# Five of the next batch's gate products moved from the mixing block into the woven block, and semaphores cleared beside later work

## The reference, cut to what matters

```python
# first mixer of a batch: projection and gate of the input x
xz = in_proj_w @ x                     # (2*1024) x 512 tokens: x part and gate part
x_part, z = split(xz)                  # z is used as silu(z), last of all
# second layer's mixer, per head, 512 steps:
kv = kt[..., :, None] * vt[..., None, :]
ot = einsum('bhk,bhkv->bhv', rt, S + bonus * kv);  S = S * dt[..., :, None] + kv
on = (o - mean) * rsqrt(var + EPS) * gn_w + gn_b
o = on * (gh * sigmoid(gh));  return o.reshape(...) @ Wo
```

## Time and profile before

| | us |
|---|---|
| median of three runs | 3989.97 (3979.78 to 3990.33) |
| profiled execution, time | 3982.17 |
| profiled execution, first to last instruction | 3980.4 |
| PE busy | 3521.7 (88%) |
| DVE busy | 3172.7 (80%) |
| ACT busy | 1609.0 (40%) |
| POOL busy | 1378.0 (35%) |
| a load of a ring slot, issue to landing, median | 4.2 |

### The profile page before, as it was taken

The page is one execution under the profiler, slowest core; times in us unless marked ns, Lnnn a source line. Parts: engine busy times, 40 slices in busy tenths (PEclk is TensorE's granted clock), DMA queues, the critical chain, the costliest instruction groups (busy, mean ns, idle before and its releaser), DMA issues. The chain is left out here.

```text
span 3980.4 us, 41707 instructions
## 1 busy us (share of the span) xinstructions
PE 3521.7 (88%) x15442; PEld 1475.8 (37%) x15442; DVE 3172.7 (80%) x2733; ACT 1609.0 (40%) x2189; POOL 1378.0 (35%) x493
## 2 busy tenths in 40 slices
PE   5777779989999979989999979989999988967999
PEld 1222243334333443334333443334433443324444
DVE  5999469887999869887999869887999869895333
ACT  5666343214655353214655353214655343213001
POOL 3454304362344304372344304372344304361000
PEclk9788899999899999989899999989899999978999
DMA  6678402121233302122233302122233302110222
GB/s 228 241 286 302 159 12 72 60 78 65 88 105 97 131 27 72 59 72 72 85 102 102 130 27 72 57 74 72 79 104 105 131 27 72 57 40 16 103 96 72
DMA packets 105431, 382.95 MB, mean 96 GB/s; under 512 B 14224, under 2 KB 27920, under 8 KB 102800
## 3 DMA queue, kind: packets, MB, share of 16 engines
q1 hardware_dynamic: 83632, 342.57, 24.6%
q10 hardware_dynamic: 21600, 37.73, 3.4%
HBM read 290.80 MB, written 64.32 MB: 89 GB/s over the span
## 5 line engine op out<-in xcount | busy, mean ns | idle before, releaser
L300 PE MATMUL ps<-r,ring 128*128 128x512 bf16 (+1 forms) x2040 | 781.4, 384 | 0.0
L297 PE MATMUL ps<-xr,ring 128*128 128x512 bf16 x1568 | 613.8, 391 | 1.4 <-PEq L2278 1.4
L301 PE MATMUL ps<-xr,ring 128*128 128x512 bf16 x1568 | 611.1, 390 | 0.0
L297 PE MATMUL ps<-r,ring 128*128 128x512 bf16 (+3 forms) x1384 | 545.4, 395 | 49.4 <-DVE xc L1102 17.8
L301 PE MATMUL ps<-r,ring 128*128 128x512 bf16 (+3 forms) x1384 | 544.8, 395 | 0.0
L1154 POOL TENSOR_TENSOR hh<-hh,bc 128x2048 f32<-128x2048 f32 x72 | 334.7, 4649 | 518.3 <-DVE hh L1064 518.3
L1154 POOL TENSOR_TENSOR bc<-bc 128x2048 f32<-128x2048 f32 x64 | 304.3, 4754 | 344.6 <-DVE bc L1064 344.6
L1154 POOL TENSOR_TENSOR r<-r,bc 128x2048 f32<-128x2048 f32 x56 | 260.9, 4658 | 297.7 <-DVE r L1064 297.7
L1064 DVE TENSOR_TENSOR_SCAN hh<-da,hh 128x2048 f32<-128x2048 f32 x72 | 325.7, 4523 | 1.3
L1105 DVE TENSOR_TENSOR xc<-xc,ps 128x512 f32<-128x512 f32 x176 | 119.5, 679 | 226.1 <-PE ps L301 225.8
L1064 DVE TENSOR_TENSOR_SCAN bc<-da,bc 128x2048 f32<-128x2048 f32 x64 | 296.0, 4625 | 0.5
(11 more groups left out here) (267 smaller groups left out, 6559.4 us busy)
## 6 DMA issues: line engine op xcount, KB each, us to landing
ring<-wsplit SPq DMA_DIRECT2D x216, 768.0 KB, 4.2
r<-wstream SPq DMA_DIRECT2D x54, 768.0 KB, 7.0
ring<-wsplit SPq DMA_DIRECT2D x76, 512.0 KB, 3.9
wsplit<-ring SPq DMA_DIRECT2D x38, 768.0 KB, 4.3
da<-r ACTq DMA_DIRECT2D x360, 63.9 KB, 2.1
wsplit<-r SPq DMA_DIRECT2D x14, 768.0 KB, 5.5
r<-wstream SPq DMA_DIRECT2D x19, 512.0 KB, 6.4
r<-xT SPq DMA_DIRECT2D x7, 1024.0 KB, 6.4
```

Source lines behind the costliest of these rows:

```text
L297: mm = pe.matmul(out, w_hi, x_hi, start=start, stop=False)
L300: pe.matmul(out, w_hi, x_lo, start=False, stop=False)
L301: return pe.matmul(out, w_lo, x_hi, start=False, stop=stop)
```

## The change

1. **Products.** The mixing block keeps 11 of the next batch's 16 products (eight projections, gates 0 to 2); gates 3 to 7 go to the woven block. There gates 3 and 4 stand where the 18 idle products were, and gates 5 to 7 where the 26 were. Behind them TensorE waits until ScalarE has taken all five. ScalarE does their curves behind the factor and ahead of the preparation's curve 2. SyncE stores them, behind the load of the second preparation slot, and ScalarE waits for the stores before it overwrites the region.
2. **Order in the scan steps.** The list of products is dealt out 3, 2, 2, 2, 3, 2, 2, 1 in place of 3, 2, 3, 3, 2, 3, 3, 3, and in group 1 two of them go ahead of the first reduce.
3. **GpSimd.** The four low parts of the next input stand behind its multiplies of groups 0 and 1, two and two, not ahead of them.
4. **Clears.** No blocks for them. A group's semaphores are cleared by SyncE alone at the start of the next block in which it streams weights, ahead of its loads; one block at the end of the kernel clears the last 41. The names carry a number, so that two groups can be held at once.

```diff
 def stream_block(k, sp, slots_end, last=NSLOTS):
+    for group, _ in k.stale:
+        for s in group:
+            sp.sem_clear(s)
+    k.idle += k.stale
+    k.stale = []
     k.w.load_until(sp, slots_end, RING - 1, last)
...
-            stream_block(k, sp, W_WO, last)
+            stream_block(k, sp, W_PROJ + 4 if ahead else W_WO, last)
...
-            work = [(value, 2), (value, 3)] + [(gate, o) for o in range(4)] + ([(ahead_product, n) for n in range(2 * J0)] if ahead else [])
+            work = [(value, 2), (value, 3)] + [(gate, o) for o in range(4)] + ([(ahead_product, n) for n in range(J0 + 3)] if ahead else [])
...
-                if g >= 1:
+                if g >= 2:
                     reduce(g - 1)
-                until = max(len(work) * (g + 1) // G, min(3, len(work)))
+                until = min(3 + 2 * g + g // 4, len(work))
...
+                if g == 1:
+                    reduce(g - 1)
...
-                for c in range(KM):
-                    low(pool, k.xn_lo[:, c, :], k.xn[:, c, :]).then_inc(nsplit, 1)
...
                 read_states(pool, g, 0, share(g)).then_inc(prod, 1)
+                if ahead and g < 2:
+                    for c in range(2 * g, 2 * g + 2):
+                        low(pool, k.xn_lo[:, c, :], k.xn[:, c, :]).then_inc(nsplit, 1)
...
-            stream_block(k, sp, W_MOE, last)
+            stream_block(k, sp, W_WO, last)
+            if ahead:
+                k.w.load_until(sp, W_WO + 2, RING - 1, last)
+                for j in range(3, J0):
+                    sp.wait_ge(gate_in, j - 2)
+                    sp.dma_start(k.gates_dram[:, j, :], k.dt0[:, j, :]).then_inc(gate_stored, 16)
+            k.w.load_until(sp, W_MOE, RING - 1, last)
...
-            keep_busy(k, pe, 0, 18)
+            if ahead:
+                gate(3)
+                gate(4)
+            else:
+                keep_busy(k, pe, 0, 18)
...
-            keep_busy(k, pe, 0, 26)
+            if ahead:
+                pe.wait_ge(cent, KM)
+                for j in range(5, J0):
+                    gate(j)
+                pe.wait_ge(gate_in, 5)
+            else:
+                keep_busy(k, pe, 0, 26)
...
             if ahead:
+                for j in range(3, J0):
+                    act.wait_ge(gate_mm, j - 2)
+                    act.activation(k.dt0[:, j, :], gate_bank(j), ACT.Silu).then_inc(gate_in, 1)
                 s.silu(act, 2)
...
                 s.take_low(act)
+                act.wait_ge(gate_stored, 5 * 16)
...
-                with nc.Block() as blk:
-                    @blk.gpsimd
-                    def _(pool):
-                        for s in held[0::4]:
-                            pool.sem_clear(s)
...
+            for _, done in k.idle:
+                done.close()
+            k.idle = []
+            k.stale.append((held, own))
...
+        with nc.Block() as blk:
+            @blk.sync
+            def _(sp):
+                for group, _ in k.stale:
+                    for s in group:
+                        sp.sem_clear(s)
```

More of the change, by code:

```diff
@@ L1489, in mix_batch @@
         bon, bv, osum, own_prod, gsplit, nsplit = sems("bon", "bv", "osum", "own_prod", "gsplit", "nsplit")
-        stored = sems("stored0", "stored1", "stored2", "stored3")
+        stored, = sems("stored")
         blk = ctx.enter_context(nc.Block())
@@ L1689, in _ @@
                     act.activation(k.projected[:, n, :], bank(N0 + n), ACT.Copy).then_inc(taken, 1)
-                for j in range(J0):
+                for j in range(3):
                     n = N0 + J0 + j
                     act.wait_ge(outp, n + 1)
-                    if j >= 4:
-                        act.wait_ge(stored[j % 4], 16)
                     act.activation(staged(j), bank(n), ACT.Silu).then_inc(taken, 1)
                     act.wait_ge(taken, n + 1)
-                    act.dma_start(k.gates_dram[:, j, :], staged(j)).then_inc(stored[j % 4], 16)
-                for i in range(4):
-                    act.wait_ge(stored[i], 32)
+                    act.dma_start(k.gates_dram[:, j, :], staged(j)).then_inc(stored, 16)
+                act.wait_ge(stored, 3 * 16)
         @blk.gpsimd
@@ L1838, in close_batch, with gate_bank @@
         logit_bank = k.ps[:, 0, 0:64].rearrange("p (c e) -> p c e", c=4)
+        gate_mm, gate_in, gate_stored = [sem(n) for n in ("gate_mm", "gate_in", "gate_stored")]
+        def gate_bank(j):
+            return k.ps[:, {3: 6, 4: 7, 5: 4, 6: 3, 7: 2}[j], :]
         def first_rows(engine, step):
@@ L1865, in mix, with gate @@
                     mm.then_inc(mixed, 1)
+            def gate(j):
+                wt = k.w.wait(pe, W_PROJ + 3 + j // 3)
+                for c in range(KM):
+                    mm = product(k, pe, gate_bank(j), wt, (j % 3 * KM + c) * P, P, high(k.xn[:, c, :]), k.xn_lo[:, c, :],
+                                 c == 0, c == KM - 1, tell=(c == 0))
+                mm.then_inc(gate_mm, 1)
+                if j in (5, 7):
+                    k.w.done()
             for c in range(KM):
@@ L2265, in cleared, with sem @@
         def cleared(order=None):
[L2267 to L2277, removed]
-                with nc.Block() as blk:
-                    @blk.gpsimd
-                    def _(pool):
-                        for s in held[0::4]:
-                            pool.sem_clear(s)
[L2284 to L2299, removed]
+            own, held, outer = ExitStack(), [], k.sem
+            def sem(name):
+                held.append(own.enter_context(nc.semaphore(f"{name}_{turn}")))
+                return held[-1]
+            k.turn += 1
+            turn = k.turn
+            if order is not None:
+                k.w = WeightStream(wsplit, ring, [sem(f"w_landed{i}") for i in range(RING)], sem("w_used"), order)
+            k.sem = sem
+            yield
+            k.sem = outer
+            for _, done in k.idle:
+                done.close()
+            k.idle = []
+            k.stale.append((held, own))
+        k.sem, k.stale, k.idle, k.turn = None, [], [], 0
         first_slots = [*range(W_PROJ, W_PROJ + 3), W_PREP0, W_PREP0 + 1]
@@ L2349, in decoder @@
         sequence(B - 1, False)
+        with nc.Block() as blk:
[4 more added lines that the diff above has]
+                        sp.sem_clear(s)
+        for _, done in k.idle + k.stale:
+            done.close()
 def _cols(a, n):
```

## The result

The changed kernel takes 3955.85 us (median; 3953.2 to 3958.3), the kernel before 3989.49 (3979.78 to 3990.33), measured together: ratio 0.992, 95% interval 0.991 to 0.994. The profiled execution took 3953.2 us with a span of 3951.4, against 3982.2 and 3980.4. The forecast was 3949, its sum for the profiled execution 3946.4.

What follows compares the result with a forecast made beforehand. It took TensorE's late last reduction to bound the mixing block's tail, and a chain the woven block's start. 3982.2 - 29.8 - 23.4 + 17.4 = 3946.4 profiled, 3954 by median; forecast 3949, a third between; range 3929 to 3971.

Steps and rivals of the forecast that it cites:

- Part 1: Block boundaries: clears and their barriers leave the path, hidden in SyncE's queue; 29.8 us saved.
- the cover: Feed-forward scan block: 12.8 us of slack in the queued load hides 79 clears (4.4 us) on SyncE.
- Part 2: Mixing block's scan: TensorE relieved of five products, GpSimd's multiply earlier; 7.8 us gained in each of three batches, 23.4.
- a share of 5.97: Mixing block: TensorE's first reduction waited 5.97 us for GpSimd's first multiply, behind low parts that the change moves.
- Part 3: Woven block: moved gates and their curves delay the first mixer product by 5.8 us, 17.4 lost over three batches.
- All behind it is one chain: Woven block: everything behind the mixer is one chain, so the mixer's 5.8 us delay is lost in each batch.
- One sign of being wrong: Time between successive woven block starts: 897.6 us before, 888 expected; over 893 would show the forecast wrong.
- 1 (the detour is hidden): Rival in the woven block: it hides its detour, the 5.8 us fall away, 3929.0 us; chance 0.11.
- 2: Rival in the mixing block: TensorE, or its clock, stays last and nothing is gained there; 3969.8 us, chance 0.14.
- 3: Rival on the clears: SyncE's serial run of clears makes loads late in most blocks; 3976.2 us, chance 0.07.
- 4: Rival in the scan steps: TensorE's clock falls to 0.5 throughout, making the kernel slower; 4030 us, chance 0.05.

Runs made afterwards that it cites:

- staggered: The changed kernel plus a block ahead of batches 0 to 2 in which SyncE clears an unused semaphore 20, 40 and 60 times; 3977.2 us, ratio 0.997.
- clears_only: The kernel before with only the clears moved as in the change; 3952.4 us, ratio 0.990.
- moves_only: The changed kernel with the clears as in the kernel before; 3988.5 us, ratio 1.001.
- after: The changed kernel itself, measured beside the kernel before; 3955.9 us, ratio 0.992.
- curve_first: The changed kernel with the preparation's curve 2 on ScalarE ahead of the five gate curves; 3928.8 us, ratio 0.985.
- thick_mixes: The changed kernel with one idle product after each of the twelve products of the mixing block's first three mixes; 3989.7 us, ratio 1.001.

## Why the forecast was 7 us low

The sum for the profiled execution was 3946.4, it took 3953.2. That the two are so near is in part luck: terms that were off by +16.5 and by -9.7 us stand against each other. Term by term:

**Part 1, the clears: right, with a gain beside it that no term had.** -29.8 forecast, -30.1 measured, and the cover held: 79 clears ahead of a load cost the feed-forward block nothing. The layer norm at the start of each batch was another 1.7 us shorter, 6.8 in all, at a clock of 1.00 for 0.89. It is 13.2 us in all four batches of every kernel without the clearing blocks except staggered, whose pauses of 2.95 and 3.66 us bring it back to 14.9 and 15.6; so it hangs on TensorE's idle time ahead of it, though its pause of 1.39 us (2.43 us idle) does nothing. clears_only gave 34.6 of median; it too has clock effects in both directions.

**Part 2, the scan: right in mechanism, small by 2.3 us a batch.** -7.8 forecast, -10.1 measured (83.3 to 73.2). moves_only, where the first half is as before, had 8.6 to 8.8. The other 1.4 are in the first step: in moves_only GpSimd's low parts of the gate's input still run beside the first scan (5.26 us), in after they were over by then and it took 4.42. The low parts of the next input, for which I took 0.8 us, cost nothing that shows. The Trainium skill, "SBUF — State Buffer", section "Who interferes with whom", has the later of the two engines wait for the whole instruction; the trace agrees: VectorE's read, begun at 1736.21 beside the multiply that ends at 1737.68, takes 2.54 us, 1.07 of them after that end. But the pairs of low parts lie beside products that read PSUM, which take their usual 2.28 us. What was wrong here is the reason from the earlier trace rows: with TensorE relieved, GpSimd's order was worth 0.3 us a batch, not a share of 5.97; the relief of TensorE is what counts, and the order only matters while sixteen products stay.

**Part 3, the woven chain: right to the mixer, wrong behind it.** The mixer was put at 26.2 us and came at 26.0; gate curves, curve 2, low part and heads came within 0.3 us of the forecast. The mixer, put at 12.3 us because of the idle time ahead of it, took 12.5 in batches 0 and 1. "All behind it is one chain" that shifts as a whole was wrong: behind VectorE's first sum these two batches took 59.6 us for 58.5, at a clock of 0.86 for 0.88. In batch 2 the mixer was at 1.00, took 10.9, and the block was 5 us shorter (93.1), so the three together were +14.9, not +17.4. No run shows why this one batch escaped. And where the mixer comes earlier, as in curve_first, it isn't the chain at all: VectorE's taps are.

**The term that is missing** rests on a step that isn't written: that code which is not edited keeps its length. The first halves of the mixing blocks took +12.7 us together, at a clock of 0.81 to 0.85 for 0.90, the unedited blocks +3.8 (-6.8 in the four layer norms, +10.6 elsewhere). These 16.5 us, less 6.9 of Part 2, 2.5 of Part 3 and 0.3 of Part 1, are the 6.8. staggered shows that such lengths change with the time at which the code runs, without an edit of it. One sign of being wrong was met by this: from one woven block's start to the next, 888 us were expected and over 893 was the sign; it was 890.9 and 893.9.

**Rivals.** 1 (the detour is hidden) didn't happen in after; curve_first made it happen (its woven blocks are 90.3 to 91.0 us, before had 91.5), at 3928.8 where it was priced at 3929.0; that the numbers agree is in part luck, for its first halves are 4.6, 1.0 and 4.6 us longer than before's and its scans 10.1, 9.6 and 10.1 shorter, where 0 and 7.8 were costed. 2 didn't happen: TensorE is relieved in the scan, and that moves_only gains nothing is because the woven blocks give all of it back (26.2 us won, 26.6 lost). 3 and 4 didn't happen either: the cover held, and the scan's clock was 0.96.

## What to carry to other kernels

Work that is moved into an idle engine isn't free if its results go through a queue on the path: place the small step that others wait for (curve 2) ahead of the bulk (five gate curves) in each queue it shares. Serial bookkeeping between barriers is worth more than its share looks: nothing hides it, and the code behind it can run at a lower clock (here 1.7 us more per batch). Where TensorE's clock varies, cost an edit with a band for the unedited code: here a few us of shift moved blocks by up to 5 us each, so a change of under some 10 us is best read from its own stretch and not from the total.

## What the runs showed of the hardware

- The same instructions took 23.6 or 28.4 us (norm and steps), 17.8 or 19.6 (the small quantised product), 52.9 to 58.4 (first half of the mixing), with a different granted clock (0.86 or 0.69 in the first) and the other engines' busy time nearly the same. Pauses of 8.0 us cost 21.3.
- A clear took 0.056 us of SyncE's queue, beside other work without a trace of a cost there.
- Behind idle time of 3.86 us the next 12.1 to 13.7 us of products ran at a clock of 0.78 to 0.89 in 14 blocks of 15, and idle products in it kept it at 1.00 in three of three. Behind the clearing blocks (2.0 to 2.8 us idle) the layer norm at the start of a batch ran at 0.88 or 0.89 in eight cases of eight, without them (1.0 us idle) at 1.00. Yet in thick_mixes TensorE, busy without a gap, stood at 0.50 for 23.9 us, and idle products made it longer. The Trainium skill, "TensorE: Matmul & The Clock Gate", section "What's actually happening", says that activity releases the throttle; the first trace agrees, the second doesn't.
